# Router products of the third x tile in the fold, W0 loads ahead of stores, a rounded bias row, a 240-column adapter, joined D0

## What is computed

```python
x = x + L0_ffn(L0_cond(x, lang_ids, ...), ...)
x = x + L1_ffn(L1_cond(x, slot_ids, ...), ...)
# L0_cond: x W0^T + 2 * sum over the two best of 8 experts of gate * (x A0_e^T) B0_e   (gates: softmax, biased by language)
# L0_ffn:  z = [router logits (8) | x A^T (128)]; the best expert alone, scaled by its logit: wh; out = wh Bw
# L1_cond: x W1^T + b1 + 2 * (x A_slot) B_slot      (one adapter slot per batch)
# L1_ffn:  x F^T + b_base + 2 * sum over the two best of 8 experts of gate * (x A1_e^T) B1_e
```

## Time and profile before

| | |
|---|---|
| median of 3 executions | 457.0 us (456.4 to 457.55) |
| the profiled execution | 457.89 us on the device; its span from first to last instruction 456.1 us |
| busy | PE 443.6 us (97%), PEld 412.5 (90%), DVE 306.9 (67%), ACT 155.0 (34%), POOL 68.7 (15%) |
| chain that ended last | PE 86%, DVE 8%, DMA 3% |
| granted TensorE clock | 1.000 over the span |

### The profile page before, as it was taken

The page is one execution under the profiler, slowest core; times in us unless marked ns, Lnnn a source line. Parts: engine busy times, 40 slices in busy tenths (PEclk is TensorE's granted clock), DMA queues, the critical chain, the costliest instruction groups (busy, mean ns, idle before and its releaser), DMA issues.

```text
span 456.1 us, 7819 instructions
## 1 busy us (share of the span) xinstructions
PE 443.6 (97%) x2750; PEld 412.5 (90%) x2750; DVE 306.9 (67%) x917; ACT 155.0 (34%) x326; POOL 68.7 (15%) x61
## 2 busy tenths in 40 slices
PE   4999989999999999999999999999999999999997
PEld 4889989999998998899999999999999999999986
DVE  3859577889943978398377558638837755863852
ACT  5656363213132552233233233314324323321310
POOL 1000000000013321301402302221040240220110
PEclk9999999999999999999999999999999999999999
DMA  7965751101110201112104102111210410300202
GB/s 260 328 222 213 234 197 46 47 0 48 52 47 1 65 9 49 47 63 102 47 19 146 49 1 109 56 45 63 100 47 17 149 46 3 113 5 1 109 2 92
DMA packets 16863, 37.08 MB, mean 81 GB/s; under 512 B 2615, under 2 KB 8761, under 8 KB 16830
## 3 DMA queue, kind: packets, MB, share of 16 engines
q1 hardware_dynamic: 16734, 36.66, 23.5%
q0 software_dynamic: 96, 0.00, 0.0%
HBM read 27.07 MB, written 9.59 MB: 80 GB/s over the span
## 4 chain that ended last, share of the span: by engine, by line
PE 86%; DVE 8%; DMA 3%; issue 1%; ACT 1%; SPq 1%; DVEq 0%; ACTq 0%
PE banks L1345 27%; PE banks L1347 27%; PE banks L1346 27%; DVE G L861 2%; PE banks L1583 2%; DMA w0s_lo_raw<-in_W_dram 1%; DMA WbTlo_raw<-in_F_dram 1%; PE banks L1353 1%; PE banks L1366 1%; DVE left L861 1%; SPq L332 1%; DVE ws_lo L861 0%; PE banks L1354 0%; PE banks L1492 0%; DVE G_raw L1121 0%
## 5 line engine op out<-in xcount | busy, mean ns | idle before, releaser
L1345 PE MATMUL banks<-G,left 128*128 128x460 f32 x224 | 88.0, 393 | 0.0
L1346 PE MATMUL banks<-G,left 128*128 128x460 f32 x224 | 82.9, 370 | 0.0
L1347 PE MATMUL banks<-G,left 128*128 128x460 f32 x224 | 82.8, 370 | 0.0
L1345 PE MATMUL banks<-WbThi,ws_hi 128*128 128x460 f32 (+1 forms) x192 | 68.0, 354 | 6.4 <-DVE WbTlo L861 5.6
L517 POOL TENSOR_TENSOR xTlo<-x_raw,xThi 128x512 fp32r<-128x512 f32 x28 | 37.9, 1373 | 200.4 <-DVE hg L919 107.4
L1347 PE MATMUL banks<-WbThi,ws_lo 128*128 128x460 f32 (+1 forms) x192 | 66.6, 347 | 0.0
L1346 PE MATMUL banks<-WbTlo,ws_hi 128*128 128x460 f32 (+1 forms) x192 | 66.4, 346 | 0.0
L569 ACT ACTIVATE left<-x_raw 128x512 fp32r<-128x512 f32 x64 | 38.8, 629 | 59.9 <-DVE x_raw L1007 29.3
L1345 PEld LDWEIGHTS banks<-WbThi,ws_hi 128*128 128x128 f32 x192 | 37.6, 196 | 10.0 <-issue 7.1
L1345 PEld LDWEIGHTS banks<-G,left 128*128 128x128 f32 x224 | 42.4, 189 | 4.5 <-DVE wzTlo L861 0.3
L1347 PEld LDWEIGHTS banks<-G,left 128*128 128x128 f32 x224 | 42.1, 188 | 4.7
(11 more groups left out here) (204 smaller groups left out, 958.0 us busy)
## 6 DMA issues: line engine op xcount, KB each, us to landing
x_raw<-in_xT_dram SPq DMA_DIRECT2D x16, 512.0 KB, 3.9
out_dram<-ybuf SPq DMA_DIRECT2D x14, 512.0 KB, 2.7
WbTlo_raw<-in_F_dram SPq DMA_DIRECT2D x8, 460.0 KB, 8.7
x_raw<-in_W_dram SPq DMA_DIRECT2D x6, 512.0 KB, 3.3
ws_lo_raw<-in_W_dram SPq DMA_DIRECT2D x3, 512.0 KB, 4.1
w0s_lo_raw<-in_W_dram SPq DMA_DIRECT2D x2, 512.0 KB, 4.8
Fbuf<-fe_hi_dram SPq DMA_DIRECT2D x16, 64.0 KB
ws_lo_raw<-in_W_dram SPq DMA_DIRECT2D x3, 256.0 KB, 5.2
```

The lines of the kernel that those rows point to most:

```text
L1345: pe.matmul(out_, l[0], r[0], start=start, stop=False, **kw)
L1346: pe.matmul(out_, l[0], r[1], start=False, stop=False, **kw)
L1347: return pe.matmul(out_, l[1], r[0], start=False, stop=stop, **kw)
```

## The change

1. `W0_HOME`: tiles 6 and 7 swap places. SP's order becomes: tiles 3, 4, 5; then the two stores that stood between them; tile 6 (waits for the product that used its new place); then the wait for the stores and tile 7. ACT's `c0_half_part(1)` and DVE's `c0_add(1)` stand ahead of the split of W1's row block 2.
2. D0hi and D0lo lie side by side in `D0T`; `add_lora0` becomes two products of 272 and 136 columns into p0 columns 136 to 407. Before them DVE clears the upper half (`clear_z`), after them ACT copies that half to SBUF (`z_part`) and DVE adds both halves (`top1`). PE waits for `z_clear`, in slots 1 to 6 ahead of `small0(a)` in place of `x1_sum`.
3. The bias row: ACT rounds `b_acc` in three parts into `b_hi`, DVE makes the remainder, and PE multiplies ones with both halves as fp32r.
4. `small0(2)`, `gates0(2)`, the turn of hg and `add_lora0(2)` move from slot 0 into the fold's end: ahead of chunk (1,1), behind it, and between chunks (0,2) and (1,2). On DVE `s_sums` 0, 1 and 2 and `s_part` 0 move ahead of `add_ident(K - 1)`, `s_part` 1 behind B21; on ACT `s_part` 0 and 1 move likewise.
5. `Ebuf` has 240 columns, `adapter` multiplies all of them, `Fbuf` loses its first 104 columns and `lora(t, half, 0)` its product with it.
6. In slot 0 `keep_p167` stands ahead of the `x1_add`s; in slot 6 `lora(m+1, 1, 0)` and `(m+1, 1, 1)` stand behind the last `ffn0`.

```diff
-        W0_HOME = [..., (b0hi, b0lo, b0raw), w0_own, xT_second, w0_ws[1]]
+        W0_HOME = [..., (b0hi, b0lo, b0raw), w0_own, w0_ws[1], xT_second]
...
             load_w0(3)
-            store_fe(1)
             sp.wait_ge(d0w_done, 1)
             load_w0(4)
-            store_fe(2)
             sp.wait_ge(c0_used, 1)
             load_w0(5)
+            store_fe(1)
+            store_fe(2)
+            sp.wait_ge(c0_used, 3)
+            load_w0(6)
             sp.wait_ge(fe_stored, 96)
-            load_w0(6)
-            sp.wait_ge(c0_used, 3)
             load_w0(7)
...
+            def z_part(t):
+                wait_earlier(act, wh_ready, t)
+                hi_half(z0_done, t + 1, z_sum[:, :], z_lo, z_rest)
...
             act.wait_ge(acc_step, 1 + 6 * K)
+            for c in range(2):
+                keep(bias_split(c)[0], bias_split(c)[2], bsum_hi)
             xT_part(2, 0, x_raw[1], x2_in[0], 16)
...
                 if c == 2:
                     a_part(0, 0, 0)
+                    exp0(2)
+                    hgT_part(2)
                 act.wait_ge(bias_done, c + 1)
...
                 s_part(b, turn, 2)
+                if has_a:
+                    z_part(a)
                 hsT_part(m, 0)
...
+            def clear_z():
+                dve.memset(z_lo, 0.0).then_inc(z_clear, 1)
...
-                dve.wait_ge(z0_done, t + 1)
-                dve.tensor_copy(GT["lg"][:, :], p0[:, z:z + E]).then_inc(lgt_ready, 1)
+                dve.wait_ge(z_rest, t + 1)
+                dve.tensor_tensor(z_sum[:, :], p0[:, ER + E:C0C], z_sum[:, :], ALU.add).then_inc(lgt_ready, 1)
+                if clear:
+                    clear_z()
...
                 if c == 2:
                     a_part(0, 0, 0, 0)
                     add_ident(LAST)
+                    gates0(2, 1)
+                    hgT_part(2)
...
             a_part(0, 0, 1, 2)
             a_part(0, 0, 3, 3)
+            s_sums(0, 0, (0, 1))
+            s_part(0, 0, 0)
+            s_sums(0, 0, (2,))
             add_ident(K - 1)
...
             lo_right(3, B21, m_psum(1, 1), g3_lo)
-            s_sums(0, 0, (0, 1))
-            def first_sums():
-                s_part(0, 0, 0)
-                s_sums(0, 0, (2,))
+            s_part(0, 0, 1)
...
                 if has_a:
+                    if b == 0:
+                        keep_p167(b)
                     for g in range(3):
                         x1_add(q, g, raw, X1W[g])
+                    dve.wait_ge(x1_sum, q * 4 + 3)
+                    clear_z()
                     a_part(q, 1 - turn, 0)
-                keep_p167(b)
+                if b > 0:
+                    keep_p167(b)
...
-                three(p0[:, ER + E:C0C], (hgThi[:, :], hgTlo[:, :]), (D0hi[:, :], D0lo[:, :]), False, True,
-                      skip_group_check=True).then_inc(z0_done, 1)
+                pe.wait_ge(z_clear, t + 1)
+                with_both(p0[:, ER + E:C0C + RC], (hgThi[:, :], hgTlo[:, :]), D0T[:, :], False, True).then_inc(z0_done, 1)
...
-                pe.matmul(bias_psum(c), ones[:, :], b_acc[:, c0:c0 + n], start=True, stop=True).then_inc(bias_done, 1)
+                hi, low, _ = bias_split(c)
+                pe.matmul(bias_psum(c), ones[:, :], hi, start=True, stop=False)
+                pe.matmul(bias_psum(c), ones[:, :], low, start=False, stop=True).then_inc(bias_done, 1)
             bias_part(0)
             bias_part(1)
+            pe.wait_ge(z_clear, 3)
+            small0(2, main_tile, 4)
             pe.wait_ge(m_kept, 4)
             m_chunk(1, 1)
+            turn_small(hg_ready, 3, pt_hg, hg[:, :], thg_done)
             pe.wait_ge(brow_lo, 1)
+            pe.wait_ge(bsum_lo, 3)
             bias_part(2)
             m_chunk(0, 2)
+            add_lora0(2)
             m_chunk(1, 2)
...
-                    pe.matmul(y, hsT[half][:, :], Fbuf[:, s], start=False, stop=True, skip_group_check=True)\
-                      .then_inc(lora_done, 1)
+                    if part:
+                        f = slice((part - 1) * w, part * w)
+                        ins = pe.matmul(y, hsT[half][:, :], Fbuf[:, f], start=False, stop=True, skip_group_check=True)
+                    ins.then_inc(lora_done, 1)
...
-                    pe.matmul(zd[half][:, R:ZC], hsT[half][:, :], Ebuf[:, :], start=False, stop=True,
+                    pe.matmul(zd[half][:, R:DW], hsT[half][:, :], Ebuf[:, :], start=False, stop=True,
...
-                        if g < 2:
+                        if g < 2 and has_n:
                             lora(m + 1, 1, g)
+                    if not has_n:
+                        lora(m + 1, 1, 0)
+                        lora(m + 1, 1, 1)
```

More of the change, by code:

```diff
@@ L56, in adaln_ffn @@
         BwTlo, BwTraw = twin("BwTlo", [P, D])
-        D0hi = sb("D0hi", [P, RC], F32R)
-        D0lo, D0raw = twin("D0lo", [P, RC])
-        Ebuf = sb("Ebuf", [96, RC], F32R)
+        D0T, D0Traw = twin("D0T", [P, 2 * RC])
+        D0hi, D0lo, D0raw = D0T[:, 0:RC], D0T[:, RC:2 * RC], D0Traw[:, RC:2 * RC]
+        z_sum = sb("z_sum", [P, RC])
+        Ebuf = sb("Ebuf", [96, DW - R], F32R)
         asraw = sb("asraw", [P, K, R])
@@ L105, in adaln_ffn @@
         with ExitStack() as fold:
-            b_acc = sb("b_acc", [P, MC], where=fold)
+            b_lo, b_acc = twin("b_lo", [P, MC], fold)
             with ExitStack() as second_tile:
@@ L134, in adaln_ffn @@
         right_factors(3)
-        Fbuf = sb("Fbuf", [96, D], F32R)
+        Fbuf = sb("Fbuf", [96, 2 * SW], F32R)
         slot_late = sb("left3", [P, 2, KH * P], F32R)
         xs = [sb("xThi", [P, D], F32R), sb("xTlo", [P, D], F32R)]
-        slot_early = [sb(f"left{i}", [P, 2, KH * P], F32R) for i in (4, 5)]
+        slot_early = [sb("left4", [P, 2, KH * P], F32R)]
+        with ExitStack() as late:
+            b_hi = sb("b_hi", [P, 2, 400], F32R, late)
+        slot_early.append(sb("left5", [P, 2, KH * P], F32R))
         x_raw = [x_raw0, x_raw1]
@@ L258, in adaln_ffn, with bias_split @@
         BIAS_PARTS = [(0, 400, 0), (400, 400, 5), (800, MC - 800, 0)]
+        def bias_split(c):
+            c0, n, _ = BIAS_PARTS[c]
+            return b_hi[:, c % 2, 0:n], b_lo[:, c0:c0 + n], b_acc[:, c0:c0 + n]
         def bias_psum(c):
@@ L440, in _ @@
             for p, src in blocks[0:2]:
-                sp.dma_start(Ebuf[p + R:p + R + 1, :].bitcast(F32), src[P:P + 1, 0:RC]).then_inc(e_in, 16)
+                sp.dma_start(Ebuf[p + R:p + R + 1, :].bitcast(F32), src[P:P + 1, 0:DW - R]).then_inc(e_in, 16)
             sp.wait_ge(m_done, m_count(LAST, 2))
@@ L805, in slot @@
                     s_part(b, turn, 1)
-                if has_a:
+                if isinstance(b, int) and b == 0:
+                    xT_part(a + 1, 1, x_raw[1 - turn], x2_in[1], 16)
+                elif has_a:
                     exp0(a)
[L808 to L814, removed]
+                    xT_part(a + 1, 1, x_raw[1 - turn], x_in[1], b * 16)
                     hgT_part(a)
@@ L965, in gates1, with top1 @@
                 spread(wz[:, :], zd[half][:, R + E:ZC], G1["g"]).then_inc(wz_ready, 1)
-            def top1(t):
+            def clear_z():
+                dve.memset(z_lo, 0.0).then_inc(z_clear, 1)
+            def top1(t, clear=True):
                 TOP = 3
@@ L1213, in _ @@
             b_times(5, 8)
-            top1(1)
+            top1(1, clear=False)
             fold_rows(3)
@@ L1276, in slot @@
                 raw = x_raw[1 - turn]
-                if has_a:
-                    gates0(a, q, first_sums if b == 0 else None)
-                s_part(b, turn, 1)
+                if b > 0:
+                    if has_a:
+                        gates0(a, q)
+                    s_part(b, turn, 1)
                 hs_part(m, 0)
-                if has_a:
+                if has_a and b > 0:
                     hgT_part(a)
@@ L1308, in slot @@
                 if has_a:
-                    top1(a + 1)
+                    top1(a + 1, clear=False)
                 wzT_part(m + 1)
@@ L1382, in first_tile, with main_tile @@
                 return lambda k: (rows(xT_first[t][0], k), rows(xT_first[t][1], k))
+            def main_tile(k):
+                return rows(xs[0], k), rows(xs[1], k)
             def m_steps(par, c, k0, k1):
@@ L1503, in _ @@
             pe.wait_ge(bias_step, 3)
-            def main_tile(k):
-                return rows(xs[0], k), rows(xs[1], k)
             def slot(b, turn, has_a, has_n, first=False):
@@ L1592, in adapter @@
                     pe.wait_ge(e_in, b * 48 + 48 + 32)
-                    pe.matmul(zd[half][:, R:ZC], hsT[half][:, :], Ebuf[:, :], start=False, stop=True,
+                    pe.matmul(zd[half][:, R:DW], hsT[half][:, :], Ebuf[:, :], start=False, stop=True,
                               skip_group_check=True).then_inc(z1_done, 1)
-                if has_a:
-                    pe.wait_ge(x1_sum, b * 4 + 3)
+                if has_a and not first:
+                    pe.wait_ge(z_clear, a + 1)
```

57 lines of the change are left out of this document (39 added, 18 removed).

## The result

The changed kernel takes 459.5 us (median of 20 executions, 457.56 to 461.8) where the kernel before takes 457.1 (20 executions): a ratio of 1.0043, 95% interval 1.0028 to 1.0058, some 2.0 us slower. The forecast was 455.1.

A forecast was written before the change was run, and what follows sets the result against it. PE's products were taken as the bound. Terms: -1.2 W0, -0.2 fold's D0, +1.9 fold's end and slot 0, -1.9 slots 1 to 6, -0.1 slot 7, -0.4 into slot 7: -1.9, to 455.1 us; range 451.8 to 457.7.

The forecast's parts named there:

- W0, -1.2: W0 stage: with the stores behind tile 5, tiles 4 and 5 land earlier; gain 1.2 us, ends 0.5 and 1.7.
- Rival (c): W0 stage: tile 7, loaded only after the moved stores land, sets its end, so no gain; 456.3 us, chance 0.07.
- The fold's end and slot 0, +1.9: Fold's end: new 3.4 us PE wait at step 8; slot 1 starts 1.9 us later, ends +0.8 and +3.2.
- Rival (b): Fold's end: clock falls in the new step 8 wait, +2.8 to +5.3 us, taken as +4: 459.1 us, chance 0.1.
- D0 -0.2: Fold's end: the two `add_lora0` with joined D0 products save 0.2 us.
- Slots 1 to 7: Slots 1 to 6 save 0.3 us each, 1.9 together; the wait before slot 7 goes, 0.4; slot 7 saves 0.1.
- D0 and adapter: Slots: joined D0 products save 0.09 us each time, 16 times; the adapter's product on 240 columns costs 0.04 more.
- Fbuf's 0.11: Slots: dropping Fbuf's 104-column product saves 0.11 us each time, 16 times.
- Rival (d): Slots: small products cost by the column, so neither D0 nor Fbuf gains; 457.3 us, chance 0.05.
- The clear, ACT's copy and the wider add: Slots 1 to 6: 0.35 us more fits into 0.54 before PE turns wh; without that cover, up to 0.3 a slot.
- Rival (a): Fold's end: no wait at step 8, as DVE reaches B22 before 161.6; 451.8 us, chance 0.15.

The follow-up runs named there:

- the order alone: The kernel before with only the change's W0 load and store order and tile homes: 458.9 us, ratio 1.0024.
- the old order: The changed kernel with W0 loads and stores, and the homes of tiles 6 and 7, as before: 457.5 us, ratio 1.0015.
- the sums behind: The changed kernel with the first slot's three sums and two splits back behind B21's remainder, on DVE and ACT: 455.9 us, ratio 0.9986.
- both edits: The changed kernel with W0 order and homes as before, and the first slot's sums and splits back behind B21's remainder: 453.7 us, ratio 0.9925.
- busy W0 wait: The changed kernel with the first slot's sums back behind B21's remainder, plus 14 unread products ahead of tile 6's: 455.1 us, ratio 0.9955.
- busy wait: The changed kernel with 32 extra products of 128 columns, results unread, ahead of step 8: 458.2 us, ratio 1.0022.

## Why the prediction was wrong

The forecast of -1.9 was a sum of six terms; two failed, and they account for the difference as closely as it can be told.

**W0, -1.2: the step that failed first.** "Tile 6 is issued some 1.4 us earlier ... but queues behind them" was right (57.16 less the 1.05 by which this execution was late at tile 3's issue is 56.1, against 57.47). What I made of the queue was not: the sum gave that place behind the stores no price. Tile 6 took 4.7 to 5.7 us from issue to split in every profile with the stores ahead of it, 3.4 in every one without stores near it, so it now lands later than before (62.86 less 1.05, against 60.89), while PE, with tile 4's wait gone, gets there earlier. I had rows for both numbers, 5.7 and 3.4, and applied the difference to tile 4 only. Tile 5 was to land some 2 us earlier and came 0.6 earlier (59.14 less 1.05, against 58.69), so its wait stayed; why it takes 5.8 us with no store ahead of it stays open. On top comes the clock behind the longer wait. Rival (c) had a loss of the gain, but by tile 7, and no cost beyond it. Measured is +1.1 (the order alone), +1.3 (the changed kernel against the old order) or +2.8 (the same pair with the sums behind).

**The fold's end and slot 0, +1.9: right but for the clock.** Split of the third bias part, step 0 and step 8 came within 0.4 us of the forecast, and the wait was 3.6 us where 3.4 stood. The step that failed is the clock, put at nothing in this term. Rival (b)'s mechanism is what went beyond it: I gave the fall a chance of 0.1, and all 32 executions of the two kernels with this wait and an idle PE read 0.996 or less, with the fall at step 8 in both profiles. Its price was less than the +2.8 to +5.3 that I had put to it: 1.5, because only some 17 of the 24 products behind it are at the lower level, and the clock is back by the time of the main products. From the last product with R0T to slot 1 the changed kernel takes 135.7 us, before 132.4: +3.4, where the terms for this stretch (D0 -0.2 and +1.9) were +1.7. The clock's 1.5 is the difference. The Trainium skill, "TensorE: Matmul & The Clock Gate", The HAM clock gate, which I had named beside the rival, says that an idle array goes to half rate; here the trace agrees, with 0.50 granted in 170 to 172.

**Slots 1 to 7: right.** From slot 1's start to slot 7's 222.6 us instead of 225.0, -2.4 where -1.9 and -0.4 stood; slot 7 -0.3 where -0.1 stood. D0 and adapter measured 0.10 and 0.04 where the forecast had 0.09 and 0.04; with Fbuf's 0.11, twice a slot, they make 0.34 of the 0.35 by which a slot got shorter. Rival (d) falls: the joined D0 does gain, and the isolated gap that the same page gives is not what these products cost. The clear, ACT's copy and the wider add are covered, as foretold.

**The sum** with the two terms put right: -1.9 + 1.5 (clock) + 2.4 (W0 at +1.2 instead of -1.2) = +2.0, and +2.0 was measured. That it closes so well is partly the choice of +1.2: with the +2.8 it would be +3.6. Rival (a) fell with the wait. The range reached to 457.7 because (b) was left out of it; with (b) in, at its own 459.1, it would still have missed the 459.5, as W0's sign was wrong too.

What stays open: why the profiled executions of some kernels have a second wait for WbTlo in the start-up. SP's loads there are the same in both kernels. Of the 50 executions of the kernel before in the two groups 7 also read a mean clock of 0.996 or less; none of them has a profile, and the start-up, where two profiles show the clock at 0.50 behind a second wait of 2.2 us, is one place where they may have lost it.

## What to carry to other kernels

Ask of a wait not only how long it is, but whether PE's clock holds through it: the clock held through three waits of 0.5 us in all three profiles that have them, while one of 1.3 to 1.7 us cost its length and often 1 to 1.6 us of slow products behind it. Where such a wait can't be removed, products whose results nobody reads can keep the clock up in it, as two runs showed; no run shows what splitting it would do. And when a store is moved out of one load's way, write down which load it now stands before, with the landing time that the trace shows for a load behind stores.

## What the runs showed of the hardware

- The clock need not fall in the wait itself. In the changed kernel it fell when PE was already at work again, 1.7 us after the wait of 1.6 us in the W0 stage and about 1 us after the one of 3.6 us at step 8, which itself shows 1.00 (165 to 168). In the wait of 4.8 us for tile 7 it fell about 1 us before the wait's end. So a full clock in the wait does not tell that the products behind it will be fast.
- A wait of 0.8 us at step 8 did not bring it down: all 16 executions of the two kernels with that wait and, behind the start-up, no longer idle one (both edits; busy W0 wait) read 0.999 or 1.000. With an idle wait of 1.3 to 1.7 us in the W0 stage 7, 8 and 9 of 12 executions read 0.996 or less (sums behind; W0 order alone; busy wait), with those of 3.6 and 4.8 us all of 32 and all of 6; of the kernel before, without any of them, 7 of 50.
- Products whose results nobody reads kept it up: 32 of 128 columns in the 3.6 us wait (1.00 from 165 to 170 in its profile), 14 in the 1.7 us one (0.999 or more in 10 of 10 executions).
